# Order of the values and the queries at the group boundaries of a cross-attention

## The reference

```
x:   [64, 32, 512]     ctx: [64, 257, 384]      16 heads of 64
q = layernorm(x) @ w_q;  k = ctx @ w_k;  v = ctx @ w_v
attn = softmax(q k^T / 8)
x = x + (attn @ v) @ w_o + b_o
x = x + self_attention(layernorm(x));  x = x + ffn(layernorm(x))
```

## Time and profile before

| what | value |
| --- | --- |
| median of 3 runs | 1573.8 us (1573.73 to 1573.83) |
| the profiled execution | 1573.89 us, of which 1571.9 us are the span from the first to the last instruction |
| granted TensorE clock | 1.00 |
| PE busy | 1557.2 us |
| DVE busy | 1226.9 us |
| ACT busy | 1035.9 us |
| POOL busy | 818.9 us |

### The profile page before, as it was taken

How to read it: one execution, slowest core, us unless ns; L and a number is a source line. 1 busy time by engine, 2 the same in 40 slices (tenths; PEclk the granted TensorE clock), 3 DMA queues, 4 the chain that set the end, 5 groups by cost and what they waited for, 6 DMA issues and landing times. The chain is left out here.

```text
span 1571.9 us, 30367 instructions
## 1 busy us (share of the span) xinstructions
PE 1557.2 (99%) x11066; PEld 1371.4 (87%) x11066; DVE 1226.9 (78%) x2410; ACT 1035.9 (66%) x2037; POOL 818.9 (52%) x784
## 2 busy tenths in 40 slices
PE   9999999999999999999999999999999999999998
PEld 7889899898998989989899888998898888888886
DVE  6558878888788887888788686677687788888887
ACT  3457777777777777777778542444444777868675
POOL 3318648476574765737546232143433555555554
PEclk9999999999999999999999999999999999999999
DMA  8984536446364563644534485332334831203010
GB/s 252 272 265 147 174 113 191 135 158 180 113 184 133 159 183 109 191 128 145 141 99 124 133 293 177 128 89 95 108 122 152 297 102 48 85 34 97 8 53 27
DMA packets 212051, 221.88 MB, mean 141 GB/s; under 512 B 84736, under 2 KB 156736, under 8 KB 211904
## 3 DMA queue, kind: packets, MB, share of 16 engines
q1 hardware_dynamic: 211904, 219.95, 45.5%
HBM read 158.02 MB, written 61.87 MB: 140 GB/s over the span
## 5 line engine op out<-in xcount | busy, mean ns | idle before, releaser
L79 PE MATMUL p_bank_score<-p_ctxt,p_qo 128*128 128x256 f32 x2304 | 304.5, 286 | 1.0 <-ACT p_probs L1117 0.6
L79 PEld LDWEIGHTS p_bank_score<-p_ctxt,p_qo 128*128 128x128 f32 x2304 | 288.1, 191 | 6.2 <-issue 2.4
L79 PE MATMUL p_bank_mix<-p_probt,p_ctx 128*128 128x512 f32 x1152 | 292.0, 398 | 0.5
L79 PEld LDWEIGHTS p_bank_mix<-p_probt,p_ctx 128*128 128x128 f32 x1152 | 207.4, 189 | 41.9 <-issue 3.8
L1321 DVE SCALAR_TENSOR_TENSOR p_qo<-p_bank_mix,p_odd,p_qo 128x512 fp32r<-128x512 f32 x192 | 143.8, 749 | 57.8 <-ACT p_qo L1131 50.2
L1131 ACT ACTIVATE p_qo<-p_bank_mix,p_odd 128x512 fp32r<-128x512 f32 x192 | 132.5, 690 | 68.3 <-PE p_bank_mix L79 67.7
L1117 ACT ACTIVATE p_probs<-p_bank_score,p_small 128x257 f32<-128x257 f32 x256 | 121.7, 476 | 58.6 <-DVE p_small L1302 54.1
L806 POOL TENSOR_SCALAR p_probs<-p_probs,p_small 128x256 f32<-128x256 f32 x256 | 122.1, 484 | 69.7 <-DVE p_small L1308 69.6
L800 POOL TENSOR_TENSOR p_ctx<-p_ctx_in,p_ctx 128x768 fp32r<-128x768 f32 x64 | 118.3, 1848 | 67.1 <-ACT p_ctx L1106 66.8
L795 POOL TENSOR_TENSOR p_ctx_in<-p_ctx_in,p_odd_in 128x768 f32<-128x768 f32 x64 | 118.2, 1846 | 39.7 <-DMA p_odd_in<-in_ctx_dram 39.7
L1302 DVE TENSOR_REDUCE p_small<-p_bank_score 128x1 f32<-128x257 f32 x256 | 105.6, 416 | 10.3 <-PE p_bank_score L79 7.6
(11 more groups left out here) (305 smaller groups left out, 3898.5 us busy)
## 6 DMA issues: line engine op xcount, KB each, us to landing
p_blocks_in<-in_ctx_dram SPq DMA_DIRECT2D x256, 96.0 KB, 2.4
p_ctx_in<-in_ctx_dram SPq DMA_DIRECT2D x64, 384.0 KB, 3.1
q<-p_ctx SPq DMA_DIRECT2D x64, 256.0 KB, 3.6
ffn<-p_w_raw SPq DMA_DIRECT2D x64, 256.0 KB, 2.8
p_odd_in<-in_ctx_dram SPq DMA_DIRECT2D x64, 192.0 KB, 3.6
p_x<-in_x_dram SPq DMA_DIRECT2D x32, 256.0 KB, 3.9
p_quad<-q SPq DMA_DIRECT2D x32, 256.0 KB, 3.7
p_probt<-q SPq DMA_DIRECT2D x32, 256.0 KB, 3.7
```

What stands on the lines that cost most here:

```text
L79: made = e.matmul(out, lhsT, rhs, start=n == 0, stop=n == last)
```

## The change

In the list of steps of a boundary the values of the fourth head tile (numbered 3) go ahead of the queries of the third (numbered 2). Nothing else is edited; the numbers of the bank uses and all semaphore counts follow from the list.

```diff
         for g in range(NG + 1):
             uses, order = [], []
-            for kind, t in (("o", 0), ("o", 1), ("q", 0), ("q", 1), ("o", 2), ("q", 2), ("o", 3), ("q", 3)):
+            for kind, t in (("o", 0), ("o", 1), ("q", 0), ("q", 1), ("o", 2), ("o", 3), ("q", 2), ("q", 3)):
                 if kind == "o" and g > 0:
                     order.append((kind, t, len(uses)))
                     uses += [(kind, ((g - 1) * NT + t) * 2 + i) for i in range(2)]
```

## The result

The changed kernel takes 1576.97 us (median of 14 runs, 1576.80 to 1577.39) against 1573.79 us for the kernel before (14 runs): ratio 1.0019, 95% interval 1.0012 to 1.0027. That is 3.2 us slower. The forecast was 1576.9.

What follows compares the result with a forecast made beforehand. TensorE, busy 99% of the span, was taken as the bound; -0.40 (block changes) + 0.44 (bank waits) + 0.40 (tail) = +0.44 us a boundary, times seven +3.1, giving 1576.9 us, range 1573.9 to 1578.3.

Steps and rivals of the forecast that it cites:

- step 2: Third and fourth tiles' queries in one run: TensorE waits for banks behind VectorE's subtractions, costing 0.44 us a boundary.
- Step 1: TensorE's changes between value and query blocks: four instead of six a boundary, gaining 0.40 us.
- step 3: Tail before the softmax: VectorE's longer backlog delays the first maximum, exponential and fourth scores, costing 0.40 us a boundary.
- A: Rival, faster: only the fewer changes of block on TensorE count, 7 x -0.40 = -2.8 us, 1571.0; chance 0.07.
- B: Rival, no change: the tail before the softmax is covered, 7 x +0.04 = +0.3 us, 1574.1; chance 0.10.
- C: Rival, slower still: GpSimd becomes last before the exponential, 7 x 0.61 = +4.3 us, 1578.1; chance 0.09.
- D: Rival: the edit does nothing because some engine keeps the old order; no chance of note.

Runs made afterwards that it cites:

- e5: Changed kernel with VectorE's five subtractions for the third head tile's queries cut to a quarter of their columns at seven boundaries: 1576.65 us, 1.0018 against the kernel before.
- e10: Kernel before, with the second unit of the first head tile's queries also given to GpSimd at the seven boundaries: 1573.43 us, ratio 0.9999.
- e2: Kernel before, reordered so the only run of two query tiles stands last, with six changes of block as before: 1576.59 us, ratio 1.0019.
- e8: Changed kernel with VectorE's maximum of the first tile's scores put ahead of its last query subtraction: 1572.71 us, 0.9993 against the kernel before.
- e7: Kernel before, with VectorE's maximum of the first tile's scores put ahead of its last query subtraction: 1571.75 us, ratio 0.9988.
- e4: Kernel before, with all four value blocks ahead of all four query blocks at a boundary: 1583.0 us, ratio 1.0059.
- e12: Changed kernel, maximum ahead of the last subtraction, second units of the first and third tiles' queries on GpSimd: 1575.13 us, 1.0009 against the kernel before.

## Why the prediction was right

**The sum** was +0.44 us a boundary and +3.1 us in all; the trace has 0.44 (97.98 against 97.54 us a group) and the runs 3.18 us. The prediction gave its own error as about 1 us. That it came within 0.1 us is in part luck: its account of the waits was wrong (step 2), which cost nothing only because the blocks were taken with their whole lengths.

**Step 1** (changes of block, -0.40): o2 with o3 came out 0.18 us shorter. What joining q2 and q3 saves shows in e5, where the run has no bank waits: 4.51 us against 4.67 apart, 0.16 less. So the two changes of block are worth some 0.35, not 0.40. No run changed their number alone. Inside a value block, matmuls of the shapes 128*128 and 128*64 take turns and still start every 0.119 us, so there the trace shows no such cost.

**Step 2** (bank waits, +0.44): the length of the run, 4.91 us, was read from q0 and q1 and came out to the hundredth, with the late start where it was expected. The waits in it are 4.91 - 4.51 = 0.40 us, not 0.44; since the run was taken whole, what step 2 had too much made up for what step 1 had too much. What the prediction said of the waits was wrong twice. They aren't a backlog of subtractions at 0.60 us each: with one subtraction less (e10) the first late start goes, but TensorE is through no sooner, since the fourth unit's subtraction waits for its copy, and only a shorter subtraction (e5) frees the bank in time. And they aren't a price of their own in this kernel: without them (e5) the time is lower by only 0.3 us, since the copies on ScalarE go on at 0.48 us each and TensorE waits at the fourth scores instead. The sum came out right because step 3 was measured from the end of the waits, so that the two add up to the length of the one chain.

**Step 3** (tail, +0.40): 3.12 us against the 3.13 foretold, fourth scores at 4.29 against 4.28, through the releaser that was named. e2 has this term alone and measures +2.84 us of the change's 3.2. e8 takes most of it away, together with the wait that was there before, and gives 4.25 us back; in the order of before the same edit gives 1.95 us (e7), so 2.3 us of the change's loss hang on the tail, and 0.10 us a boundary of it is left in e8.

**The rivals.** A (only the changes of block) is refuted by the change itself and by e4, which has the fewest changes and is the slowest. B (the tail covered) is refuted by e2 and e8. C (GpSimd last) didn't occur in the change, where GpSimd ends at 222.10, 2.73 us after the scores began; in e12 it did. D (some engine keeps the old order) is refuted by the windows of the changed kernel, in which the blocks stand in the new order.

## What to carry to other kernels

All this is shown for one kernel. Where TensorE fills PSUM faster than two engines empty it, what counts is which block stands last before work that needs those engines: a slow block between two fast ones lets them catch up, and at the end a run of two fast ones lays its backlog on the path of the first maximum and exponential. If the profile already has the same run elsewhere in the loop, take its time whole, with its end measured from its start, and don't price the waits inside it apart from the backlog behind it. And before reordering, look at what one engine does in order in the tail: the maximum moved ahead of one subtraction gave more (1.95 us) than any order of the blocks.

## What the runs showed that was not expected

Taking work off the engine that looked like the bound of the run (VectorE, 0.60 us a subtraction against 0.48 a copy) freed nothing in e10, and shortening its subtractions gave 0.3 of 5.9 us expected in e5. The early units of a run wait for their copies anyway, and a bank is free only when copy and subtraction have both been made.

A short wait of TensorE cost more than its length. The interval behind it was some 0.07 us too long, which is why e7 gave 0.28 us a boundary for a wait of 0.21.
